# Cross-attention scores from high and low halves of queries and keys, with the key projection moved ahead of the query's

## The reference, cut to what matters

```
xn = layernorm(x)
q = (xn @ Wq.T + bq).reshape(B, 64, 16, 16)
k = (ctx @ Wk.T + bk).reshape(B, 256, 16, 16)
v = (ctx @ Wv.T + bv).reshape(B, 256, 16, 16)
scores = einsum('blhe,bshe->bhls', q, k)
out = einsum('bhls,bshe->blhe', softmax(scores * 16 ** -0.5), v)
x = x + out @ Wo.T + bo
```

## Time and profile before

| | |
|---|---|
| median of 3 runs | 958.99 us (954.76 to 959.69) |
| the profiled execution | 959.17 us, span of the trace 957.4 us |
| mean granted TensorE clock | 0.988 |
| PE busy | 896.8 us, 94% |
| DVE busy | 788.0 us, 82% |
| ACT busy | 689.3 us, 72% |
| POOL busy | 343.2 us, 36% |

### The profile page before, as it was taken

The page is one execution under the profiler, slowest core; times in us unless marked ns, Lnnn a source line. Parts: engine busy times, 40 slices in busy tenths (PEclk is TensorE's granted clock), DMA queues, the critical chain, the costliest instruction groups (busy, mean ns, idle before and its releaser), DMA issues. The chain is left out here.

```text
span 957.4 us, 29217 instructions
## 1 busy us (share of the span) xinstructions
PE 896.8 (94%) x9714; PEld 726.8 (76%) x9730; DVE 788.0 (82%) x1711; ACT 689.3 (72%) x1983; POOL 343.2 (36%) x487
## 2 busy tenths in 40 slices
PE   5999999999999999999999988999999996999997
PEld 4788888888888888888888876777777773555554
DVE  3778878888888888878878868888888886999997
ACT  3677776777767777677776756776777665988887
POOL 1322223222232222333323237566666631222221
PEclk9999999999999999999999989999999997999999
DMA  8111111111111111111111000000000000000001
GB/s 301 36 38 39 44 39 34 40 39 44 38 33 38 39 44 38 33 38 39 44 38 34 21 1 2 1 2 0 1 0 1 2 1 1 28 28 28 28 28 39
DMA packets 31618, 31.64 MB, mean 33 GB/s; under 512 B 3280, under 2 KB 30800, under 8 KB 31568
## 3 DMA queue, kind: packets, MB, share of 16 engines
q1 hardware_dynamic: 30720, 30.73, 10.4%
q10 hardware_dynamic: 848, 0.33, 0.1%
HBM read 26.86 MB, written 4.19 MB: 32 GB/s over the span
## 5 line engine op out<-in xcount | busy, mean ns | idle before, releaser
L485 ACT ACTIVATE probs<-psum,nmax 128x256 f32<-128x256 f32 x512 | 237.2, 487 | 89.5 <-DVE nmax L445 89.5
L445 DVE TENSOR_REDUCE nmax<-psum 128x2 f32<-128x512 f32 x256 | 158.9, 683 | 30.2 <-PE psum L315 30.2
L328 PE MATMUL psum<-id_sb,probs 128*128 128x128 f32 x1024 | 137.2, 278 | 14.1 <-ACT probs L485 14.0
L328 PEld LDWEIGHTS psum<-id_sb,probs 128*128 128x128 f32 x1024 | 113.0, 142 | 29.8 <-ACT probs L485 28.3
L493 POOL TENSOR_TENSOR rstd<-vare,minus_half 128x1 f32<-128x1 f32 x96 | 52.7, 549 | 199.8 <-DVE vare L382 197.3
L502 POOL TENSOR_TENSOR cl<-c_sb,ch 128x512 fp32r<-128x512 f32 x64 | 81.5, 1274 | 99.8 <-ACT ch L460 99.8
L485 ACT ACTIVATION_READ_ACCUMULATOR probs<-psum,nmax 128x1 f32 x512 | 112.4, 219 | 0.0
L466 ACT ACTIVATE probsT<-psum 128x512 f32<-128x512 f32 x160 | 90.8, 621 | 11.4 <-PE psum L328 11.4
L509 POOL TENSOR_TENSOR rm<-rinv,hm_sb 128x256 f32<-128x256 f32 x64 | 39.7, 620 | 127.6 <-DVE rinv L421 127.6
L315 PE MATMUL psum<-k_sb,qb 32*128 32x256 f32 x1024 | 78.5, 403 | 0.0
L1006 PE MATMUL psum<-wb_all,xqT 128*128 128x512 bf16 x240 | 66.4, 391 | 10.4 <-DVE probs L906 7.1
(11 more groups left out here) (126 smaller groups left out, 2304.6 us busy)
## 6 DMA issues: line engine op xcount, KB each, us to landing
c_sb<-in_ctx_t SPq DMA_DIRECT2D x64, 256.0 KB, 2.7
x_sb<-in_x SPq DMA_DIRECT2D x32, 128.0 KB, 2.0
out<-y_sb SPq DMA_DIRECT2D x32, 128.0 KB, 1.7
w_all<-in_w_gate SPq DMA_DIRECT2D x1, 1024.0 KB, 7.7
w_all<-in_w_up SPq DMA_DIRECT2D x1, 1024.0 KB, 9.8
w_all<-in_w_down SPq DMA_DIRECT2D x1, 1024.0 KB, 12.3
wqkv_sb<-in_w_qkv SPq DMA_DIRECT2D x1, 768.0 KB, 6.6
wq_sb<-in_wq ACTq DMA_DIRECT2D x1, 256.0 KB, 3.7
```

What stands on the lines that cost most here:

```text
L328: last = nc.tensor.transpose(sp[g][:, c:c + P], probs[:, 2 * g + u, kh * P:(kh + 1) * P], id_sb[:])
L445: nc.vector.tensor_reduce(nmax[:, 2 * g:2 * g + 2], sp[g].rearrange("p (u s) -> p u s", u=2), AX.X, ALU.max, negate=True).then_inc(max_don ...
L485: nc.scalar.activation(probs[:, j, :], sp[g][:, u * S:(u + 1) * S], ACT.Exp, bias=nmax[:, j:j + 1], accum_out=rsum[:, j:j + 1]).then_inc(e ...
```

## The change

Queries and keys are split as the context already was. ACT writes their rounded high halves (`act_qh`, `act_kh`: `qh`, `kh_sb`), DVE the query's low half (`dve_ql`), POOL the key's (`pool_kl`). The scores become three float32r products over the same four row tiles: qh·kh, qh·kl and ql·kh. `pe_scores` now waits for `ql_done` and `kl_done` instead of `qb_done` and `k_ev`. All new tiles are single buffers, so `act_kh` and `act_qh` also wait for the scores that read them last. In PE's body `pe_k(t + 1, 0)` moves ahead of `pe_q(t + 1)` and `pe_r(t, 0)`; in DVE's body `dve_k(t + 1, 0)` moves from behind the probability copy to ahead of `dve_q`. To make room, `kbd4`, a buffer of the self attention, is laid over `w_all`, with a wait on POOL for the last rounding step.

```diff
+        qh, ql = sb("qh", [P, KT, 2, 2, L], F32R), sb("ql", [P, KT, 2, 2, L], F32R)
+        kh_sb, kl_sb = sb("kh_sb", [P, KT, S], F32R), sb("kl_sb", [P, KT, S], F32R)
...
-        kbd4 = [sb(f"kbd4{s}", [P, KT, 4, P]) for s in range(2)]
+        kbd4 = [w_all[:, 2 * i:2 * i + 2, :].rearrange("p k (h t) -> p k h t", h=4) for i in range(2)]
...
-            pe.wait_ge(qb_done, t * 4 + 4)
-            pe.wait_ge(k_ev, b + 1)
+            pe.wait_ge(ql_done, t + 1)
+            pe.wait_ge(kl_done, b + 1)
             for m in range(KT):
...
+                for n, (q, k) in enumerate(((qh, kh_sb), (qh, kl_sb), (ql, kh_sb))):
+                    for c in range(4):
...
+                        last = nc.tensor.matmul(sp[c][:, m * S:(m + 1) * S],
+                                                q[rows, m, s, :, :].rearrange("p h q -> p (h q)"),
+                                                k[rows, m, :], start=n == 0, stop=n == 2)
...
+        def dve_ql(v, t):
+            v.wait_ge(qh_done, t + 1)
+            flat = "p m s h q -> p (m s h q)"
+            nc.vector.tensor_tensor(ql[:].rearrange(flat), qb[:].rearrange(flat),
+                                    qh[:].rearrange(flat).bitcast(F32),
+                                    ALU.subtract).then_inc(ql_done, 1)
...
+        def act_qh(a, t):
+            a.wait_ge(qb_done, t * 4 + 4)
+            a.wait_ge(s_mm, t * 8)
...
+        def act_kh(a, t, s):
+            a.wait_ge(k_ev, t * 2 + s + 1)
+            a.wait_ge(s_mm, (t * 2 + s) * 4)
+            nc.scalar.activation(kh_sb[:], k_sb[:], ACT.Copy).then_inc(kh_done, 1)
...
+        def pool_kl(p, t, s):
+            p.wait_ge(kh_done, t * 2 + s + 1)
+            nc.gpsimd.tensor_tensor(kl_sb[:], k_sb[:], kh_sb[:].bitcast(F32),
+                                    ALU.subtract).then_inc(kl_done, 1)
...
+                    pe_k(pe, t + 1, 0)
                     pe_q(pe, t + 1)
                     pe_r(pe, t, 0)
-                    pe_k(pe, t + 1, 0)
...
+                    act_kh(a, t, 1)
                     act_pt(a, t, 0)
...
                     act_exp(a, t, 1, (t, 0))
+                    act_kh(a, t + 1, 0)
+                    act_qh(a, t + 1)
                     act_pt(a, t, 1)
...
                     pool_rstd(p, LN1, t + 1)
+                    pool_kl(p, t, 1)
                     pool_rm(p, t, 0)
                     pool_xb(p, t + 1)
                     pool_c(p, t + 1, 0)
+                    pool_kl(p, t + 1, 0)
                     pool_rm(p, t, 1)
```

More of the change, by code:

```diff
@@ L104, in block_kernel @@
         xnT = sb("xnT", [P, KT, P])
-        qb = [sb(f"qb{m}", [P, 2, 2, L]) for m in range(KT)]
+        qb = sb("qb", [P, KT, 2, 2, L])
         k_sb = sb("k_sb", [P, KT, S])
+        qh, ql = sb("qh", [P, KT, 2, 2, L], F32R), sb("ql", [P, KT, 2, 2, L], F32R)
+        kh_sb, kl_sb = sb("kh_sb", [P, KT, S], F32R), sb("kl_sb", [P, KT, S], F32R)
         v_sb = [sb(f"v_sb{s}", [P, 2, D]) for s in range(2)]
@@ L212, in block_kernel @@
         cl_done = sem("cl_done")
+        qh_done = sem("qh_done")
+        ql_done = sem("ql_done")
+        kh_done = sem("kh_done")
+        kl_done = sem("kl_done")
         k_mm = sem("k_mm")
@@ L306, in pe_scores @@
             b = t * 2 + s
-            pe.wait_ge(qb_done, t * 4 + 4)
-            pe.wait_ge(k_ev, b + 1)
+            pe.wait_ge(ql_done, t + 1)
+            pe.wait_ge(kl_done, b + 1)
             for m in range(KT):
[L310 to L319, removed]
+                for n, (q, k) in enumerate(((qh, kh_sb), (qh, kl_sb), (ql, kh_sb))):
+                    for c in range(4):
+                        if m + n == 0 and (not isinstance(b, int) or b > 0):
+                            moved, count = pt_count(t + s - 1, 1 - s, c)
+                            pe.wait_ge(moved, count)
+                        rows = slice(32 * c, 32 * c + 32)
+                        last = nc.tensor.matmul(sp[c][:, m * S:(m + 1) * S],
+                                                q[rows, m, s, :, :].rearrange("p h q -> p (h q)"),
+                                                k[rows, m, :], start=n == 0, stop=n == 2)
+                        if m == KT - 1 and n == 2:
+                            last.then_inc(s_mm, 1)
         def pe_transpose(pe, t, s, groups=range(4)):
@@ L396, in dve_k @@
             v.wait_ge(k_mm, t * 2 + s + 1)
+            v.wait_ge(kl_done, t * 2 + s)
             nc.vector.tensor_tensor(k_sb[:], k_ps, bk_sb[:].unsqueeze(2).to_broadcast([P, KT, S]),
@@ L401, in dve_q @@
             v.wait_ge(q_mm, t + 1)
-            v.wait_ge(s_mm, t * 8)
+            v.wait_ge(ql_done, t)
             for m in range(KT):
@@ L460, in act_c @@
             nc.scalar.activation(ch[s][:], c_sb[s][:], ACT.Copy).then_inc(ch_done, 1)
+        def act_qh(a, t):
+            a.wait_ge(qb_done, t * 4 + 4)
+            a.wait_ge(s_mm, t * 8)
+            flat = "p m s h q -> p (m s h q)"
+            nc.scalar.activation(qh[:].rearrange(flat), qb[:].rearrange(flat),
+                                 ACT.Copy).then_inc(qh_done, 1)
+        def act_kh(a, t, s):
+            a.wait_ge(k_ev, t * 2 + s + 1)
+            a.wait_ge(s_mm, (t * 2 + s) * 4)
+            nc.scalar.activation(kh_sb[:], k_sb[:], ACT.Copy).then_inc(kh_done, 1)
         def act_pt(a, t, s):
@@ L1188, in _ @@
                 dve_k(v, 0, 0)
+                dve_ql(v, 0)
                 v.wait_ge(w1_in, 16 * len(SET1))
@@ L1207, in body @@
                     dve_max(v, t, 1)
+                    dve_k(v, t + 1, 0)
                     dve_q(v, t + 1)
@@ L1217, in body @@
                         dve_wcast(v, piece)
-                    dve_k(v, t + 1, 0)
+                    dve_ql(v, t + 1)
                     dve_v(v, t + 1, 0)
@@ L1307, in _ @@
                 act_c(a, 0, 1)
+                act_qh(a, 0)
+                act_kh(a, 0, 0)
                 act_exp(a, 0, 0)
                 def body(t, pieces=None, w2=None):
+                    act_kh(a, t, 1)
                     act_pt(a, t, 0)
@@ L1388, in _ @@
                 pool_c(p, 0, 1)
+                pool_kl(p, 0, 0)
                 def body(t, w2=None):
                     pool_rstd(p, LN1, t + 1)
+                    pool_kl(p, t, 1)
                     pool_rm(p, t, 0)
@@ L1415, in _ @@
                 pool_xl(p, 1, 0, 1)
+                p.wait_ge(wq_step, 36)
                 pool_kbd4(p, 0, 0, 0, 0)
```

2 lines of the change are left out of this document (1 added, 1 removed).

## The result

The changed kernel takes 1009.65 us, the median of four runs (1006.59 to 1010.87), beside 958.02 of the kernel before on the same chip: a ratio of 1.0527, with a 95% interval of 1.0508 to 1.0546. It is slower, as forecast, and 1009.65 lies in the range of 976 to 1014, but 14.7 us above the 995 that I named. The profiled execution of it has a span of 1004.7 us, 47.3 more than the 957.4 of before.

What follows compares the result with a forecast made beforehand. PE was taken to bound the first half of a tile, a chain through scores, maxima, exponentials and transposes the second. Added terms of 36.9 on a 957.4 span plus 1.8 around it gave 996.1, forecast as 995, range 976 to 1014 us.

Steps and rivals of the forecast that it cites:

- rival of slow rounds: Scores on PE: float32r rounds take 0.22 us, second half takes on 0.62 us, 1014 us in all; chance 0.11.
- PE's saving: Block of scores on PE: six float32r rounds take 0.94 us instead of 1.08, saving 0.14 us.
- One sign of the forecast: Scores of (t + 1, 0): released by ACT's third copy at about 9.2, and by DVE's ql only in tiles 9 to 20.
- plus 0.69: DVE's chain in the first half: ql takes 0.69 us from 8.0 and ends at 8.7.
- 12 x 0.3 = 3.6 us: Tiles 9 to 20: weight pieces ahead of ql on DVE make it end about 0.3 us behind the banks.
- the block of 0.94 us: Scores on PE: six rounds of 0.117 us take 0.70, plus 0.24 us of filling and switching.
- The prologue: Before the loop: the first scores wait for kh (0.62) and kl (1.28), counted as 0.8 us more.
- 36.9 forecast: Whole kernel's added time: 32.6 for 31 tiles + 3.6 for pieces + 0.8 for the prologue - 0.1 for the last tile.
- the wait for R doesn't appear: First half on ACT: without the wait, qb sets qh and the half is 8.65: 15.5 us less, 979 us; chance 0.10.
- The clock rival: PE in the loop: clock falls to 1.2 GHz for part of each tile, 1030 us or above; chance 0.05, shared with missed chains.

Runs made afterwards that it cites:

- e2: Changed kernel with only the high by high product of the scores made (8 float32r matmuls instead of 24), all splits kept: 995.36 us, 1.0387.
- e6: Changed kernel with the scores as the 8 float32 matmuls of the kernel before, all splits and their waits kept: 1005.16 us, 1.0474.
- e4: Changed kernel with PE's four waits for the strips' banks moved ahead of its waits for ql and kl: 1000.09 us, 1.0427.
- e3: Changed kernel with POOL forming only 16 of the 256 keys of kl after the first batch: 991.43 us, 1.0336.
- e5: Changed kernel with PE turning rm (R) ahead of the key projection instead of behind both projections: 1018.53 us, 1.0621.
- e8: Changed kernel with both R ahead of the key projection and kl cut to 16 keys: 988.48 us, 1.0309.
- e1: Changed kernel with PE's key projection moved back behind the query projection and R, DVE's new order kept: 1045.19 us, 1.0892.

## Why the prediction was right and where it missed

**The direction and the mechanism were right, and the time only in part.** 1009.65 lies inside the range because that reaches up to 1014, and it reaches there for the rival of slow rounds, which did not happen. That the terms I had too small add up to about as much as this rival is luck. (The sum gives 995.9, which I rounded down to 995, and the chances of a slower kernel add up to 0.94, where the last line says 0.92.)

PE's saving was never the question: half of the time the loop hangs on a chain through ACT, and the change lengthens that chain. K starts at 2.47 (forecast 2.47), Q at 3.97 (3.97), ACT's `kh` at 6.45 (6.58), its copies end at 9.06 (9.18), the first half lasts 9.13 (9.15). `r_sb` waits for R, but 0.51 us and not 0.9: ACT is ready for it at 4.76 instead of 4.46, because the block of scores and the maxima behind it are 0.3 us later. The clock of ordinary tiles stays at 1.00. With fewer products (e2), other products (e6) or the waits moved (e4), the first half keeps 9.10 to 9.13, so it is not PE's matmuls that set it. That ACT's two new copies do is read from the order of time; no run leaves a copy out, and its price isn't measured by itself.

One sign of the forecast came otherwise: `ql`, and not ACT's third copy, releases the scores in ordinary tiles too. The two end 0.06 us apart (541.51 and 541.57). It is luck that the long `ql` didn't lengthen this half: it began at 7.67 where I had 8.0.

**The rounds on the row tiles** cost 0.117 us, the value I took from the key projection, and not 0.22: the rival of slow rounds falls, by the rows of the block and by e2. The loads of these rounds take 0.18 us each and are hidden in them. The traces so go against the rule of the Trainium skill that the prediction weighed ("TensorE: Matmul & The Clock Gate", Part 3).

**The first step that failed was "plus 0.69"** in `ql`'s chain on DVE. The row it came from the earlier trace rows had POOL idle. In the loop `kl` and `ql` meet by construction: both are released by ACT's `kh` and `qh`, 0.52 us apart. `ql` took 1.33, and e3 shows that POOL's instruction is the reason. In e3, with 16 keys of `kl`, it is 0.88. It also hit the pieces: a cast of 0.856 instead of 0.512, a rounding of 0.88 instead of 0.48 and a `ql` of 1.10. The term "12 x 0.3 = 3.6 us" measured 12 x 0.88 = 10.6, and 1.5 more for the clock in two of them, 8.5 us in all above the forecast. Without the full `kl` it is 12 x 0.45 = 5.4 (e3). The Trainium skill states the rule that I failed to apply ("SBUF — State Buffer", section "Who interferes with whom"): a DVE instruction with two SBUF inputs and a GpSimd instruction that reads SBUF exclude each other, as do DVE copies and scalings in its two-port modes, and the one issued later stands. The traces agree, with 1.33 beside 0.69, 0.856 beside 0.512, and `oT` with 1.00 beside 0.29 in e5.

**The second was the block of 0.94 us.** The rounds were right, but I took the four waits for the banks as met while PE still worked. Where `ql` releases PE, they come one by one: 1.23 us instead of 0.94, and the second half 9.12 instead of 8.90. This is (9.12 - 8.90) x 31 = 6.8 us. e4 removes just this and gives the forecast second half. The block of (t, 1) is staggered too in ordinary tiles (1.20 us), and there it is `kl`:

```profile
549.17 1.32 POOL L535 TENSOR_TENSOR kl_sb<-k_sb,kh_sb 128x512 fp32r<-128x512 f32 x1 [0.93 <-ACT kh_sb L488]
```

It ends 8.84 us into the second half, where I had 8.45, and 0.27 ahead of the scores. With the small `kl` of e3 these blocks take 0.91 in tiles 1 to 30.

**The sum again.** 36.9 forecast, plus 8.5 for the pieces, 6.8 for the block, less 0.6 for the first halves that were 0.02 shorter and 1.4 that the later phases gave back, makes 50.2, beside a measured 47.3. The prologue cost what I had: the first scores of (0, 1) come 0.9 us later. Of the 2.9 that are left, 2.1 lie in tile 0. I had counted its pass with the 31 longer ones, at 1.25 us more, and it takes 18.05 us instead of 18.90; before, it had a stretch at half the clock, and after, none. The rest is the base: the other 30 passes of before take 17.06 us in the mean and not 17.00.

The medians lie 51.6 apart (1009.65 - 958.02) and not 47.3, as the profiled execution was the fastest of the four of the changed kernel, and that of the kernel before was above its median.

**The rival "the wait for R doesn't appear"** was priced at 15.5 us. e5 took the wait away and came out 9 us slower, e8 gave 3. The mechanism that I named for it, that `qb` then sets `qh`, shows in e5's row; the price forgot that an earlier `kh` moves `kl` onto `oT`.

**The clock rival** had a small part in the profiled execution: two half-rate stretches behind tile 0, beside 15 in e1, nine in e5 and four in e2. All came at or behind a wait of over 1 us for `ql`, and none with PE's waits of 0.5 us. But e4 and e6 have twelve such long waits each and no stretch, so what else it takes is open. The mean granted clock was 0.990 in the profiled execution and 0.983 to 0.986 in the other three. Taking 3.4 us at half the clock for a stretch, and 0.73 us as its cost, I estimate from these means that the other three had two to four stretches more. That is 2 to 3 us of the 2.1 to 4.2 by which they are longer.

## What to carry to other kernels

When work is added to two engines at once, lay their instructions side by side in time before using a duration from a row in which the other was idle, above all for DVE with two inputs in SBUF beside GpSimd. Ask where the new block's waits are met: a chain of cheap waits behind the one that comes last is paid in full, and putting the early ones first gives it back. And where an engine only seems to be the bound, look for the gap in its chain first: here moving one projection into a gap gained 1.2%, while the shorter rounds of the scores came with splits and waits that cost 5%.

## What the runs showed of the hardware that I had not expected

Float32r matmuls of 256 columns on four row tiles start a round every 0.117 us from the second on, weight loads of the same strip included. They do so although a strip's load takes 0.18 us as in the earlier trace rows. Four semaphore waits that were already fulfilled took PE about 0.3 us where it met them behind a wait that came last (tile 12, scores of (t + 1, 0); e4 takes them away), and nothing where it didn't: the block of (t, 1) in tile 12 starts PV 0.91 us after its first round. And an instruction that is held up by another engine's shows in the profile as a longer instruction and not as a wait, so the list of waits names the wrong cause: it says that PE waits for `ql`, and only `ql`'s own duration points to POOL.
